# A selective scan on four engines: smaller pieces of side work on TensorE, single buffers for delta and du, a longer ring of states, and one more product in sixteen on GpSimd

## The reference

```
delta = softplus(dt_proj @ dt_lo + bias)
state[t] = state[t-1] * exp(delta[t] * A[e, n]) + delta[t] * u[t] * B[n, t]
y[t]     = sum over n of state[t] * C[n, t]
x = x + (y + D * u) * silu(layernorm(x))
```

## Time and profile before

| | us |
|---|---|
| median of 3 runs (lowest, highest) | 1291.56 (1291.31, 1293.41) |
| the profiled execution, its own time | 1293.37 |
| its span, first to last instruction | 1290.7 |
| busy in the span: PE, DVE, ACT, POOL | 1117.9, 755.9, 524.3, 639.3 |

### The profile page before, as it was taken

How to read it: one execution, slowest core, us unless ns; L and a number is a source line. 1 busy time by engine, 2 the same in 40 slices (tenths; PEclk the granted TensorE clock), 3 DMA queues, 4 the chain that set the end, 5 groups by cost and what they waited for, 6 DMA issues and landing times.

```text
span 1290.7 us, 19382 instructions
## 1 busy us (share of the span) xinstructions
PE 1117.9 (87%) x4940; PEld 836.3 (65%) x4940; DVE 755.9 (59%) x823; ACT 524.3 (41%) x706; POOL 639.3 (50%) x465
## 2 busy tenths in 40 slices
PE   6677778797788767738999999999999999999994
PEld 2344454465456545637788888888888888888883
DVE  5888999979987989656324343531532534324321
ACT  5955756665566554213223132421422323213210
POOL 0798999999989899304122232221321223212221
PEclk9677888878877767657999999999999999999997
DMA  6432232522432233064214353421531435215310
GB/s 208 142 104 92 84 112 76 174 85 87 129 110 90 82 112 109 0 250 174 99 41 164 106 179 113 165 105 43 179 104 35 171 108 179 105 41 171 106 47 19
DMA packets 65444, 145.08 MB, mean 112 GB/s; under 512 B 8654, under 2 KB 11214, under 8 KB 65408
## 3 DMA queue, kind: packets, MB, share of 16 engines
q1 hardware_dynamic: 56368, 116.34, 26.8%
q0 software_dynamic: 9040, 28.32, 6.7%
HBM read 320.53 MB, written 18.35 MB: 263 GB/s over the span
## 4 chain that ended last, share of the span: by engine, by line
PE 53%; DVE 2%; issue 0%; ACT 0%; POOL 0%; ACTq 0%; DVEq 0%; POOLq 0%
PE hp L1507 11%; PE hp L1506 11%; PE hp L1505 11%; PE yp L1505 5%; PE yp L1507 5%; PE yp L1506 5%; PE tp L1546 2%; PE xp L1499 1%; PE yp L1551 0%; DVE R L1343 0%; DVE S_tok L1339 0%; DVE S_w L1334 0%; DVE S_w L1447 0%; DVE S_w L1445 0%; DVE xT_lo L1402 0%
## 5 line engine op out<-in xcount | busy, mean ns | idle before, releaser
L284 POOL TENSOR_TENSOR ring<-du,bB 128x1024 f32<-128x1024 f32 x128 | 299.9, 2361 | 53.2 <-DVE du L654 36.7
L588 DVE TENSOR_TENSOR_SCAN ring<-dA,ring 128x512 f32<-128x512 f32 x256 | 296.0, 1205 | 15.4 <-ACT dA L368 9.9
L368 ACT ACTIVATE dA<-delta,Acol 128x512 f32<-128x512 f32 x256 | 172.3, 687 | 165.4 <-DVE ring L588 162.7
L1505 PE MATMUL hp<-w_hi,xT_hi 128*128 128x512 f32 x592 | 236.5, 399 | 2.1 <-DVE xT_lo L1402 2.1
L1507 PE MATMUL hp<-w_hi,xT_lo 128*128 128x512 f32 x592 | 236.2, 399 | 0.0
L1506 PE MATMUL hp<-w_lo,xT_hi 128*128 128x512 f32 x592 | 234.1, 396 | 0.0
L753 PEld LDWEIGHTS yT<-ident,ring 128*128 128x128 f32 x1024 | 146.7, 172 | 93.3 <-issue 76.2
L733 PE MATMUL Cb<-xdbl,ident 48*128 48x512 f32 x176 | 125.9, 802 | 91.8 <-DVE ring L594 91.8
L1144 POOL COPY out_index<-out_tab 128x1 uint32 x37 | 6.7, 181 | 356.5 <-DVE work L1409 356.5
L1423 DVE TENSOR_TENSOR work<-hp,work 128x512 f32<-128x512 f32 x74 | 51.1, 690 | 224.3 <-PE hp L1507 221.1
L753 PE MATMUL yT<-ident,ring 128*128 128x128 f32 x1024 | 172.8, 331 | 8.0 <-POOL ring L293 8.0
(11 more groups left out here) (202 smaller groups left out, 1403.4 us busy)
## 6 DMA issues: line engine op xcount, KB each, us to landing
stage<-in_L_ffn_w_kernel_dram SPq DMA_DIRECT2D x160, 1024.0 KB
stage<-in_L_ffn_wo_kernel_dram SPq DMA_DIRECT2D x78, 1024.0 KB
bB<-bcs SPq DMA_DIRECT2D x64, 512.0 KB, 3.6
bC<-bcs SPq DMA_DIRECT2D x40, 256.0 KB, 4.4
xall<-in_x_dram SPq DMA_DIRECT2D x1, 4096.0 KB, 14.1
xln_dram<-xlnb SPq DMA_DIRECT2D x4, 1024.0 KB, 6.8
out_dram<-xall SPq DMA_DIRECT2D x4, 1024.0 KB, 8.9
ctx_rows<-in_ctx_dram SPq DMA_DIRECT2D x4, 512.0 KB, 6.0
```

The source lines that it names most:

```text
L284: g_.tensor_tensor(ring[:, q % RING, :].rearrange("p (e l) -> p e l", e=2), dub(b, h * 2 * L, 2 * L).rearrange("p (e l) -> p e l", e=2), B ...
L368: a_.activation(dA[r % SB][:, :], db(b, eb * L, L), ACT.Exp, scale=Acol[:, eb, n:n + 1]).then_inc(exp_done, 1)
L588: v_.tensor_tensor_scan(o, dA[r % SB][:, :], o, 0.0, ALU.mult, ALU.add).then_inc(scan_done, 1)
L1505: t_.matmul(bank[:, :], a_hi[:, k, :], b_hi[:, b, :], start=(start and k == ks[0]), stop=False)
```

## The change

`POOL_C` goes from n = 2, 5, 8, 11, 14 to n = 1, 4, 6, 9, 11, 14: GpSimd makes 48 of 128 products instead of 40, VectorE 80 instead of 88, and TensorE fills `Cb` 80 times instead of 88. The ring has 12 slots instead of 8. `delta` and `du` have one buffer instead of two, and three waits are added or tightened for it. TensorE's side work is cut into single tiles or pairs on neighbouring places; the four G tiles and the logits come earlier (places 16, 17, 23, 24, then 26 and 27), the second `dt_proj` later (30 instead of 25), and `USES` is reordered to match. ScalarE copies G2 and G3 at place 25 instead of 31, and its `dt_half(b + 1, 1)` is at 31 instead of 28. VectorE copies the logits at place 29, in the last sequence too.

```diff
-RING = 8
+RING = 12
-POOL_C = (2, 5, 8, 11, 14)
+POOL_C = (1, 4, 6, 9, 11, 14)
-        delta = sb("delta", [P, 2, EB * L])
-        du = sb("du", [P, 2, EB * L])
+        delta = sb("delta", [P, EB * L])
+        du = sb("du", [P, EB * L])
-            USES += [f"{n}.{b + 1}" for n in ("XP", "DT0", "DT1", "DT2", "DT3") if nxt]
+            USES += [f"{n}.{b + 1}" for n in ("XP", "DT0", "DT1") if nxt]
             USES += [f"{n}.{b - 1}" for n in ("G2", "G3", "LG") if rest]
+            USES += [f"{n}.{b + 1}" for n in ("DT2", "DT3") if nxt]
...
# ScalarE, dt_half
-                if b > 1:
-                    act.wait_ge(du_ready, g - 3)
+                if b > 0:
+                    act.wait_ge(du_ready, g - 1)
+                    act.wait_ge(exp_done, 2 * (q0(b - 1, i) + UPH))
...
# ScalarE, the places
-                    if s == 24 and nxt:
+                    if s == 23 and nxt:
                         dt_half(b + 1, 0)
                         soft(b + 1, 0)
-                    if s == 27 and nxt:
-                        soft_log(b + 1, 0)
-                    if s == 28 and nxt:
-                        dt_half(b + 1, 1)
-                    if s == 31 and rest:
+                    if s == 25 and rest:
                         gate_T(b - 1, 2)
                         gate_T(b - 1, 3)
+                    if s == 26 and nxt:
+                        soft_log(b + 1, 0)
+                    if s == 31 and nxt:
+                        dt_half(b + 1, 1)
...
# VectorE, loss, and the places
-                if b > 1:
-                    dve.wait_ge(dbu_done, q0(b - 2, i) + UPH)
+                if b > 0:
+                    dve.wait_ge(dbu_done, q0(b - 1, i) + UPH)
...
-                if rest and nxt:
-                    logit_copy(b - 1)
+                    if s == 29 and rest:
+                        logit_copy(b - 1)
             if NU - 1 in NTH_DVE:
                 times_c(NU - 1)
-            logit_copy(NB - 2)
             drain_y(NB - 1, 1)
...
# TensorE, the places
-                    if s == 0 and nxt:
-                        ctx_T(b + 1)
-                    if s == 3 and rest:
-                        zs_T(b, (0, 1))
-                    if s == 6 and rest:
-                        zs_T(b, (2, 3))
...
-                    if s == 8 and nxt and rest:
-                        in_proj(b + 1, (0, 1))
...
-                    if s == 12 and nxt:
-                        in_proj(b + 1, (2, 3))
-                    if s == 16 and rest:
-                        gate_T(b - 1, 0)
-                        gate_T(b - 1, 1)
+                    if s in (0, 1) and nxt:
+                        ctx_T(b + 1, (s,))
+                    if s in (4, 5, 7, 8) and rest:
+                        zs_T(b, ((4, 5, 7, 8).index(s),))
+                    if s in (9, 10, 11, 12) and not rest:
+                        zs_T(b, (s - 9,))
+                    if s in ((9, 10) if rest else (4, 5)) and nxt:
+                        in_proj(b + 1, (s - (9 if rest else 4),))
+                    if s in (13, 14) and nxt:
+                        in_proj(b + 1, (s - 11,))
+                    if s in (16, 17) and rest:
+                        gate_T(b - 1, s - 16)
                     if s == 19 and nxt:
-                        x_proj(b + 1)
-                    if s == 21 and nxt:
+                        x_proj(b + 1, (0, 1))
+                    if s == 20 and nxt:
+                        x_proj(b + 1, (2, 3))
+                    if s == 22 and nxt:
                         dt_proj(b + 1, 0)
-                    if s == 25 and nxt:
+                    if s in (23, 24) and rest:
+                        gate_T(b - 1, s - 21)
+                    if s == 26 and rest:
+                        logits_of(b - 1, (0, 1))
+                    if s == 27 and rest:
+                        logits_of(b - 1, (2, 3))
+                    if s == 30 and nxt:
                         dt_proj(b + 1, 1)
-                    if s == 28 and rest:
-                        gate_T(b - 1, 2)
-                        gate_T(b - 1, 3)
-                    if s == 31 and rest:
-                        logits_of(b - 1)
```

More of the change, by code:

```diff
@@ L154, in db @@
         def db(b, lo, n):
-            return delta[:, b % 2, lo:lo + n]
+            return delta[:, lo:lo + n]
         def dub(b, lo, n):
-            return du[:, b % 2, lo:lo + n]
+            return du[:, lo:lo + n]
         def row(t, b, i):
@@ L755, in acc, with ctx_T @@
                 last.then_inc(acc_done, 1)
-            def ctx_T(b):
+            def ctx_T(b, tiles):
                 pe.wait_ge(ctx_loaded, (b + 1) * 16)
-                for i in range(KB):
+                for i in tiles:
                     o, done = use(f"T{i}.{b}")
@@ L773, in in_proj, with x_proj @@
                     last.then_inc(done, 1)
-            def x_proj(b):
+            def x_proj(b, ebs):
                 o, done = use(f"XP.{b}")
@@ L778, in x_proj @@
                     pe.wait_ge(u_ready, b)
-                for eb in range(EB):
+                for eb in ebs:
                     if b == 0:
@@ L782, in x_proj @@
                     last = t_.matmul(o[0:DR + 2 * DS, :], xpT[:, eb, :], ub(b, eb * L, L), start=(eb == 0), stop=(eb == EB - 1))
-                last.then_inc(done, 1)
+                if eb == EB - 1:
+                    last.then_inc(done, 1)
             def dt_proj(b, i):
@@ L805, in gate_T, with logits_of @@
                 last.then_inc(done, 1)
-            def logits_of(b):
+            def logits_of(b, rows):
                 for i in (LB - 2, LB - 1):
@@ L811, in logits_of @@
                 o, done = use(f"LG.{b}")
-                for i in range(LB):
+                for i in rows:
                     for d in range(DI // P):
                         last = t_.matmul(o[:, i * 8:(i + 1) * 8], gT[:, i, d * P:(d + 1) * P], gate[:, d, :], start=(d == 0), stop=(d == DI // P - 1))
-                last.then_inc(done, 1)
+                if i == LB - 1:
+                    last.then_inc(done, 1)
             def logits_row(i):
@@ L830, in _ @@
                 last.then_inc(done, 1)
-            ctx_T(0)
+            ctx_T(0, range(KB))
             in_proj(0, range(EB))
@@ L842, in _ @@
             last.then_inc(done, 1)
-            x_proj(0)
+            x_proj(0, range(EB))
             dt_proj(0, 0)
@@ L854, in _ @@
                         acc(q - LAG)
-                    if s == 0 and nxt:
-                        ctx_T(b + 1)
-                    if s == 3 and rest:
-                        zs_T(b, (0, 1))
-                    if s == 6 and rest:
-                        zs_T(b, (2, 3))
-                    if s == 4 and nxt and not rest:
-                        in_proj(b + 1, (0, 1))
-                    if s == 8 and nxt and rest:
-                        in_proj(b + 1, (0, 1))
-                    if s == 9 and not rest:
-                        zs_T(b, (0, 1))
@@ L867, in _ @@
-                    if s == 11 and not rest:
-                        zs_T(b, (2, 3))
-                    if s == 12 and nxt:
-                        in_proj(b + 1, (2, 3))
-                    if s == 16 and rest:
-                        gate_T(b - 1, 0)
-                        gate_T(b - 1, 1)
+                    if s in (0, 1) and nxt:
+                        ctx_T(b + 1, (s,))
+                    if s in (4, 5, 7, 8) and rest:
+                        zs_T(b, ((4, 5, 7, 8).index(s),))
```

## The result

The changed kernel takes 1339.78 us (median of 3, 1339.29 to 1340.33) against 1291.56: a ratio of 1.0369, 95% interval 1.0346 to 1.0393. It is 48 us slower where 12.5 us less were forecast. Its profiled execution took 1339.29 us, with a span of 1336.6. In the later comparisons the kernel before gave two groups of times, 1290.7 to 1297.2 and 1301.0 to 1305.1 us, for a reason that stays open; a ratio pools both groups, so a ratio within 1% of one has to be read with the single runs beside it.

A forecast was written before the change was run, and what follows sets the result against it. It took VectorE with its stalls as the pacing engine, GpSimd close behind and the bound after the change. Logits -8.6 and loop -3.9 (-10.9 + 7 of GpSimd idle) gave -12.5: 1279.1 us, range 1271.5 to 1287.5.

The forecast's parts named there:

- Reading: On the profile page, TensorE rises to nine tenths for good and GpSimd falls from nine to two, at about 575 us.
- Step 1: Eight products moved in the loop: GpSimd +18.5 us, VectorE -9.0 us; the extra loads of C cost 0.
- Step 2: Ring of 12: GpSimd's slot waits of 16.0 us go; between 0 and 16.0 us may come back, scans being late next.
- Step 3: End of the block: 10.7 us from last product with C to `drain_y` become 2.1; 8.6 saved, bounds 6 and 10.7.
- Step 4: Loop: GpSimd becomes the bound, gain at most 10.9 us; VectorE alone would allow an end 10 us earlier.
- the sign against itself: VectorE's waits for GpSimd, 5.6 us before, staying under 6 would mean GpSimd has not become the bound.
- Step 5, third point: Places 11 to 20, heavy for VectorE, with TensorE's work nearer ScalarE's need: 2 us of GpSimd idle, bounds 0 and 8.
- Step 6: Single buffers, ScalarE's moved blocks and the pieces of side work count as nothing, taken by 10 us of VectorE's room.
- The lock of step 5, its first point: VectorE's `loss` and GpSimd share SBUF ports: six more collisions may cost GpSimd 1.0 us each; 3 taken, bounds 0 and 6.
- step 5, second point: GpSimd's `sub_loss` waits for VectorE's `loss`, 2.27 us at a time, three times; 2 us taken, bounds 0 and 11.
- Rival C: Handing over: GpSimd idle 15 us instead of 7, places 11 to 20 and 25 holding VectorE back; 1287 us, chance 0.20.
- Rival E: Slower: GpSimd's three kinds of waits stay in full with 18.5 us more laid on it; 1297.9 us, chance 0.03.

The follow-up runs named there:

- experiment 7: Kernel before with the last sequence's logits early: 0.9971; first two copies deferred too: 0.9962; both with early pieces: 0.9963; early tail and early pieces, no deferred copies: 0.9906.
- Experiments 2 to 4: TensorE's front places undone in the changed kernel 1.0185; in the kernel before, whole blocks late 1.0242, early pieces 0.991, one place later 1.0144, ScalarE and VectorE too 1.0021.

## Why the prediction was wrong

The reading of the bound was half right: the block is where everything happens, and VectorE paced it through its stalls. The forecast then rested on VectorE and GpSimd, and the answer lay with TensorE and ScalarE, which were far from full.

- Reading: by the earlier trace rows GpSimd leaves its nines at about 515 us and TensorE reaches its own at about 613, not both at 575. The sum does not use it.
- Step 1, the eight products: the sizes were right, GpSimd's products take 112.8 us instead of 94.1. But alone the list cost 1%, 13 us, and on top of the rest nothing.
- Step 2, the ring: right that the slot waits of 16.0 us go and scans take their place. It is 43.3 us in all for scans, where at most 16.0 were allowed to come back.
- Step 3, the logits: right for the changed kernel, 10.7 us became 1.5. In the kernel before the same move did not shorten the whole by that much (experiment 7).
- Step 4, GpSimd becomes the bound, and VectorE has 10 us of room: wrong. VectorE waited 4.2 us for GpSimd, under the 6 that the prediction gave as the sign against itself, and GpSimd waited for VectorE.
- Step 5, third point, is the first half of the step that failed: "`acc(6)` on TensorE now waits for GpSimd, then the last `zs_T`, ScalarE's copy and the next exponential. Bounds 0 and 8; I take 2". The chain was named, and sized at 2 us for the whole block. The trace shows 6.19 us of it at one place of one sequence, with `acc(6)` waiting for nobody. Experiments 2 to 4 show what makes it: the distance between the places of TensorE and ScalarE (whole blocks at late places, with the old list, cost 2.4%). No row stands behind the upper bound of 8.
- Step 6 is the other half. It priced the pieces and ScalarE's moved blocks with the 9.9 us that VectorE waited for exponentials, "between all gone and doubled", and let the 10 us of room in step 4 take them, so they entered the sum as nothing. They measured 89.7 us, and the room was not there. A wait of 9.9 us was read from a trace in which the side work stood two or three places ahead of its consumer; it bounds nothing for a distance of one. Step 5 said that TensorE takes this work nearer to where ScalarE wants it, but neither step counted the places. Before, zs stood 2 places ahead of its copy, in_proj 3, x_proj 2, the first dt_proj 3, the second 3. After, the last piece of each stands 0, 1, 1, 1 and 1 ahead. TensorE's places stand in the diff, ScalarE's in the diff and the kernel. The section on the change says that the four G tiles come earlier; G0 stays at 16 and G1 moves from 16 to 17.
- The lock of step 5, its first point: three of seven `loss` took longer than their 1.2 us (2.08, 3.22 and 1.45; 1.66 on average against 1.51), and the GpSimd operation behind it was 1.0 us longer in two of them. That is 2.0 us of GpSimd where it was 0.97, and 3 more were counted on. This agrees with the rule of the Trainium skill that the prediction cites, from the page "SBUF — State Buffer", section "SBUF: two separate sides", and it did not matter for the time.
- The wait of `sub_loss` for `loss`, step 5, second point: it went from 6.8 to 20.9 us, 14.1 more where 2 were taken and 11 was the bound. It is VectorE's lateness again, seen from GpSimd.
- Rival C had VectorE held back at the heavy places, with 15 us of idle in all; GpSimd's waits for scans and for `loss` alone came to 43.3 + 20.9 = 64.2. Rival E had the sign, at 3% and for another reason: GpSimd did not pace the block. The range was too narrow because it was built from GpSimd's idle alone.

## What to carry to other kernels

Where engines run lists in order and hand over through few buffers, count for each piece of side work how many places it stands ahead of its consumer before and after a move, and look which wait stands in front of it on its own engine. If that wait depends on what the consumer gives next, the short distance closes a ring, as at place 8 here, where VectorE stood for 6.19 us. Moving the consumer by the same place took a loss of 1.4% to 0.2%. A cut into pieces should start earlier, not end later: that order lost nothing here. An engine that is half idle can still be the one whose order decides.

## What was not expected of the hardware

TensorE's granted clock was lower in the kernel in which it waited more: 0.68 to 0.73 in the three stretches, where the kernel before had 0.72 to 0.81. A fill of `Cb` took 2.07 us at place 8 where others in the same trace take 1.12, and an accumulation 1.97 against 1.09. Such slow fills are not new, only more frequent: 38 of 80 took over 2 us, and 23 of 88 in the kernel before. So late side work seems to be paid twice, once in the wait and once in the slower steps of the ring; how much of the loss is the second part, no run separates.
